# Dividing attention's sums by features: transfers and wide reciprocals in place of TensorE transposes, in a fused block of one core

## The reference

```python
x = x + 0.5 * ffn(layernorm(x))
x = x + attention(layernorm(x))
x = x + 0.5 * ffn(layernorm(x))

def attention(x):                      # 16 heads of 16 features
    q, k, v = split(lora_linear(x, Wq, ...)), split(...), split(...)
    scores = einsum('bhqd,bhkd->bhqk', q, k) * 16 ** -0.5
    attn = softmax(scores, axis=-1)
    out = einsum('bhqk,bhkd->bhqd', attn, v)
    out = merge_heads(out)             # B x 1024 x 256
    return lora_linear(out, Wo, bo, Bo, Ao)
```

## Time and profile before

| | |
|---|---|
| median of three runs | 830.17 us (829.87 to 831.24) |
| the profiled execution | 832.18 us, of which its span is 830.4 us |
| PE busy in the span | 806.1 us, 97% |
| DVE busy | 681.9 us, 82% |
| ACT busy | 474.0 us, 57% |
| POOL busy | 194.2 us, 23% |
| chain that ended last | PE 85%, DVE 8%, ACT 4%, issue 3%, DMA 1% |

### The profile page before, as it was taken

One profiled execution on the slowest core, in us unless ns is written; L12 is line 12 of the kernel. 1 busy time (PEld: TensorE's weight loads), 2 busy tenths in 40 slices (PEclk: granted clock), 3 DMA queues, 4 the chain that ended last, 5 costly groups with the idle time before them and its releaser, 6 DMA issues.

```text
span 830.4 us, 14316 instructions
## 1 busy us (share of the span) xinstructions
PE 806.1 (97%) x5424; PEld 516.8 (62%) x5424; DVE 681.9 (82%) x1127; ACT 474.0 (57%) x900; POOL 194.2 (23%) x206
## 2 busy tenths in 40 slices
PE   5989999999999999999999999999999999999997
PEld 4868788888876433333333434443358888888886
DVE  4997888787599999999999888889846977876865
ACT  4543433432432788888888888888863333333322
POOL 1450112410011033333332322143430201120100
PEclk9999999999999999999999999999999999999999
DMA  8110000000050242223333222210000000000000
GB/s 278 39 39 1 0 1 1 2 1 0 1 90 1 40 79 54 40 39 65 65 65 64 41 40 40 59 33 27 16 12 1 1 2 26 0 26 1 1 25 26
DMA packets 19333, 27.87 MB, mean 34 GB/s; under 512 B 4608, under 2 KB 13632, under 8 KB 19264
## 3 DMA queue, kind: packets, MB, share of 16 engines
q1 hardware_dynamic: 18592, 26.30, 14.5%
q10 hardware_dynamic: 672, 0.66, 0.3%
HBM read 12.09 MB, written 2.10 MB: 17 GB/s over the span
## 4 chain that ended last, share of the span: by engine, by line
PE 85%; DVE 8%; ACT 4%; issue 3%; DMA 1%; DVEq 0%; ACTq 0%; POOL 0%
PE front_ps L1668 17%; PE front_ps L1649 14%; PE max_ps L1609 6%; PE ffn_gate_ps L49 5%; PE ffn_gate_ps L51 5%; PE ffn_gate_ps L50 5%; PE ffn_out_ps L756 5%; PE ffn_out_ps L757 5%; PE ffn_out_ps L760 5%; PE ffn_up_ps L49 3%; PE ffn_up_ps L51 3%; PE ffn_up_ps L50 3%; ACT probs L1799 2%; PE ffn_mix_ps L735 2%; DVE ffn_hidden_lo L1119 1%
## 5 line engine op out<-in xcount | busy, mean ns | idle before, releaser
L1879 DVE TENSOR_REDUCE maxima<-max_ps 128x2 f32<-128x1024 f32 x256 | 311.1, 1223 | 29.3 <-PE max_ps L1609 26.8
L1799 ACT ACTIVATE probs<-front_ps 128x512 f32<-128x512 f32 x512 | 277.5, 597 | 38.9 <-PE front_ps L1649 29.1
L882 ACT ACTIVATE ffn_tanh<-ffn_gate_ps 128x512 f32<-128x512 f32 x96 | 57.4, 598 | 219.0 <-PE ffn_gate_ps L51 219.0
L1668 PE MATMUL front_ps<-probs,values 128*32 128x256 f32 x2048 | 163.4, 391 | 4.4 <-ACT mixed_t L1804 4.0
L1128 DVE SCALAR_TENSOR_TENSOR ffn_gated<-ffn_tanh,ffn_gate_ps 128x512 f32<-128x512 f32 x96 | 65.8, 685 | 61.2 <-ACT ffn_tanh L882 60.8
L1668 PEld LDWEIGHTS front_ps<-probs,values 128*32 128x32 f32 x2048 | 40.8, 108 | 95.5 <-issue 55.7
L1649 PE MATMUL front_ps<-q_stack,k_stack 49*128 49x512 f32 x256 | 94.6, 446 | 0.0
L1609 PE MATMUL max_ps<-ffn_xlo,ffn_xhi 48*128 48x512 f32 x256 | 93.9, 447 | 0.0
L1549 POOL TENSOR_TENSOR inverse_sum<-turned,minus_one 128x16 f32<-128x16 f32 x15 | 43.7, 2916 | 207.4 <-ACT turned L1811 207.4
L1649 PE MATMUL front_ps<-ffn_xhi,ffn_xlo 49*128 49x512 f32 x256 | 91.4, 455 | 0.0
L1609 PE MATMUL max_ps<-k_stack,q_stack 48*128 48x512 f32 x256 | 88.2, 455 | 0.6 <-DVE maxima L1879 0.4
(11 more groups left out here) (209 smaller groups left out, 1296.2 us busy)
## 6 DMA issues: line engine op xcount, KB each, us to landing
q_stack<-block SPq DMA_DIRECT2D x48, 64.0 KB, 2.3
ffn_xhi<-block SPq DMA_DIRECT2D x48, 64.0 KB, 2.3
ffn_xlo<-block SPq DMA_DIRECT2D x48, 64.0 KB, 2.3
k_stack<-block SPq DMA_DIRECT2D x42, 64.0 KB, 2.3
x_sb<-in_x SPq DMA_DIRECT2D x3, 512.0 KB, 9.3
out<-x_sb SPq DMA_DIRECT2D x3, 512.0 KB, 2.9
ffn_out_rows<-in_down SPq DMA_DIRECT2D x4, 256.0 KB, 5.9
weights_again<-in_gate SPq DMA_DIRECT2D x2, 512.0 KB, 3.6
```

Source lines behind the costliest of these rows:

```text
L1668: mm = pe.matmul(mixed_ps[strip:strip + STRIP, at:at + HALF // 2], values[g % SLOTS][:, kt, j, :], probs[:, (g * KEY_TILES + kt) % PROBS, ...
L1799: act.activation(probs[:, tile % PROBS, j, half * HALF:(half + 1) * HALF], score_ps[:, n % RING, :], ACT.Exp, scale=SCORE_SCALE).then_inc( ...
L1879: v.reduce_max(maxima[:, g % 2, m // 2, m % 2, :], max_ps[:, m % 2, :, :], axis=AXIS_X).then_inc(pair_max, 1)
```

## The change

The mix is no longer turned. `values` now has 16 columns of v and 16 columns of ones, so that each strip of the mix has 16 rows of features and the same sum in 16 further rows. Once the mix is copied out, SyncE issues eight transfers per group (`move_on_sync`): four bring the features' rows into `attn_out`, which now has features in its rows, and four the sums' rows to the same rows of a buffer `sums` of 128 x 1024. When four groups are there, VectorE takes the reciprocal of all the sums in one instruction, before the maxima of groups 6, 10 and 14 (`invert_on_vector`), and GpSimd multiplies (`normalize_on_gpsimd`). The last four groups are divided by VectorE in two halves of 512 columns, behind units 0 and 2 of the second FFN (`divide_last_on_vector`). The output product reads `attn_out` as it is. `turn_out`, `copy_turned`, `write_out`, `turn_on_tensor`, `columns_of` and `LastMix` go.

```diff
+    MOVES = 4
-            self.columns = sb("o_columns", [P, 2, KT, PAIR_TILES, P])
+            self.sums = sb("o_sums", [P, SEQ])
...
+    def move_on_sync(self, sp, g, mixed):
+        sp.wait_ge(self.mixed_out, g + 1)
+        for half in range(2):
+            at = slice(half * HALF, (half + 1) * HALF)
+            for j in range(2):
+                strip, to = (j * 2 + half) * 2 * HD, (g % SLOTS * 2 + j) * HD
+                sp.dma_start(self.rows_of(g)[to:to + HD, at], mixed[strip:strip + HD, :]
+                             ).then_inc(self.moved[half], 16)
+                sp.dma_start(self.sums[to:to + HD, at], mixed[strip + HD:strip + 2 * HD, :]
+                             ).then_inc(self.moved[half], 16)
+    def invert_on_vector(self, v, s):
+        for half in range(2):
+            self.wait_moved(v, half, (s + 1) * SLOTS)
+        v.reciprocal(self.sums[:, :], self.sums[:, :]).then_inc(self.inverted, 1)
+    def normalize_on_gpsimd(self, pool, s):
+        rows = self.rows_of(s * SLOTS)
+        pool.wait_ge(self.inverted, s + 1)
+        pool.tensor_tensor(rows, rows, self.sums[:, :], ALU.mult).then_inc(self.normalized, 1)
+    def divide_last_on_vector(self, v, half):
+        at, before = slice(half * HALF, (half + 1) * HALF), GROUPS // SLOTS - 1
+        rows = self.rows_of(GROUPS - 1)[:, at]
+        self.wait_moved(v, half, GROUPS)
+        v.reciprocal(self.sums[:, at], self.sums[:, at]).then_inc(self.inverted, 1)
+        v.wait_ge(self.inverted, before + half + 1)
+        v.tensor_tensor(rows, rows, self.sums[:, at], ALU.mult).then_inc(self.normalized, 1)
...
# second FFN: TensorE, ScalarE, VectorE
         def output_product(p):
-            pe.wait_ge(project.columns_done, p + 1)
+            pe.wait_ge(project.normalized, GROUPS // SLOTS + p // 2)
...
-            if u == 0 and not first:
-                pe.wait_ge(rows_out, JT // 2 - 1)
-                last.turn_on_tensor(pe, out_ps[:, 0, :], ident[:, :])
-            if pair_beside(u, 0) in (0, 1):
-                turn_attention(pair_beside(u, 0))
...
-            last.write_on_vector(v)
             v.wait_ge(keep["x_biased"], CHUNKS)
         for u in range(UNITS_ALL):
             unit(u)
             if u:
                 low_part(u - 1)
+            if not first and u in (0, 2):
+                project.divide_last_on_vector(v, u // 2)
...
# attention: SyncE
+            def move_out(g):
+                if g % SLOTS == 0:
+                    sp.wait_ge(values_in, g + SLOTS)
+                    if g:
+                        sp.wait_ge(project.normalized, g // SLOTS)
+                project.move_on_sync(sp, g, mixed[:, :])
             for g in range(GROUPS - 1):
+                if g:
+                    move_out(g - 1)
...
+            for g in (GROUPS - 2, GROUPS - 1):
+                move_out(g)
# attention: TensorE and ScalarE
-                    if kt == OUT_TURN_AT and g:
-                        turn_out(g - 1)
...
-                    if kt == TURN_ROWS_AT and 0 <= g - FIRST_PAIR_AT < NORM_PAIRS:
-                        attention_rows(g - FIRST_PAIR_AT)
...
             def copy_mixed(g):
                 act.wait_ge(probs_used, (g + 1) * KEY_TILES)
+                if g:
+                    for half in range(2):
+                        project.wait_moved(act, half, g)
# attention: VectorE and GpSimd
             for g in range(GROUPS):
+                if g % SLOTS == 2 and g > SLOTS:
+                    project.invert_on_vector(v, g // SLOTS - 1)
...
+                if g % SLOTS == SLOTS - 1:
+                    project.normalize_on_gpsimd(pool, g // SLOTS)
```

More of the change, by code:

```diff
@@ L750, in down @@
                     pe.wait_ge(rows_out, JT // 2)
-                    pe.wait_ge(last.copied, 1)
             x_hi, x_lo = hidden_hi[:, u % SPLIT_RING, :], hidden_lo[:, u % SPLIT_RING, :]
@@ L924, in _ @@
                 raw.copy_update_on_scalar(act, 2, update_banks[2])
-            if u == 0 and not first:
-                last.copy_on_scalar(act, out_ps[:, 0, :])
             for c, i in routing_beside(u - 1):
```

147 lines of the change are left out of this document (26 added, 121 removed).

## The result

| | kernel before | changed kernel |
|---|---|---|
| median of the runs, us | 830.02 (829.77 to 831.24, 4 runs) | 880.99 (869.87 to 891.32, 4 runs) |
| ratio, undisturbed runs | | 1.0492, 95% interval 1.0472 to 1.0513 |
| profiled execution, us | 832.18 | 869.87 |
| its span, mean granted clock of TensorE | 830.4, 0.996 | 868.0, 0.954 |

The change costs 40 us or more, where 21.3 were forecast and the range ended at 864. The direction was right, the size was not. The four executions of the changed kernel took 869.87, 873.13, 888.85 and 891.32 us at a mean granted clock of 0.954, 0.953, 0.930 and 0.928.

What follows compares the result with a forecast made beforehand. TensorE was taken to set the pace in attention and the second FFN. Terms -11.4 + 17.5 + 7.5 + 5.2 + 2.5 = +21.3 us gave a median of 851.5 us, likeliest case 846 to 857, 8 in 10 839 to 864.

Steps and rivals of the forecast that it cites:

- point 3: Attention: after each of the three long pauses TensorE's clock halves, costing 2.5 us each, 7.5 us lost; bounds 0 and twice that.
- point 4: Second FFN: waits for the half reciprocals lose 5.2 us net of turns gone; one clock drop adds 2.5 us.
- the clock stays up: Rival: no clock loss in attention or the second FFN, so +11.3 us, 841.5 us; chance 0.17.
- Point 1: Attention: the transposes go, 0.60 us each time on TensorE, 19 times, 11.4 us gained.
- SyncE itself is not late: Attention: SyncE's eight issues end some 13 us after the group's start, the maxima's rows are issued 17.9 us after it.
- Point 2: Attention, groups 4, 8 and 12: VectorE's reciprocals of 1024 columns take 6.6 us each; 6.5, 6.2 and 4.8, together 17.5 us lost.
- The half microsecond per group: Opening, attention: VectorE, busy 19.64 of 21 us, was said to have about half a microsecond per group to spare.
- the plain rate: Rival: a reciprocal of 1024 columns runs at the plain rate, 1.2 us, giving -9.7 us, 820.5 us; chance 0.08.
- eight slots to a column: Rival: at 8.3 ns per column a reciprocal of 1024 columns takes 8.6 us, giving 859 us; chance 0.10.
- The transfers that land late: Rival: transfers land after 4.6 us instead of 2.3, three waits in attention and one in the FFN grow, 860 us; chance 0.10.

Runs made afterwards that it cites:

- e7: e6 with the last four groups divided in quarters of 256 columns, behind units 0, 3, 11 and 20 of the second FFN: 823.34 us, ratio 0.9919.
- e3: Kernel before, with two idle reciprocals of 512 columns of ones on VectorE before the maxima of groups 6, 10 and 14: 873.58 us median.
- e6: Changed kernel, sums of groups 0 to 11 moved once, inverted by one reciprocal of 64 columns per four groups, repeated through DRAM: 828.62 us, ratio 0.9983.
- e2: Changed kernel with each of attention's three reciprocals cut into eight pieces of 128 columns, one behind every second reduction: 877.91 us median, ratio 1.0548.
- e12: Changed kernel with 24 products of the 128x128 identity on TensorE ahead of one score in groups 4, 8 and 12: 845.84 us median, ratio 1.0189.
- e11: Changed kernel with the first score of key tile 6 done twenty-five times on TensorE in groups 4, 8 and 12: 874.62 us median, ratio 1.0484.

## Why the forecast was right in sign and wrong in size

**The step that failed is point 3, the clock**, and with it the clock's part of point 4. The mechanism was right, and the size of this term was not. It said "I count 2.5 after each: 7.5 us", from one pause in the first FFN, with 0 and 15 us as its ends. In the profiled execution of the changed kernel the clock was low for 61 us in attention (24, 17 and 20, summed over windows of 2 us). Some 10 of these lay in the stops themselves, where TensorE had nothing to lose; 19, 15 and 17 us came after it had its work back. A step then took 2.16 us instead of 1.24, so a share of 0.43 is lost, which gives 22 us.

The same can be measured directly, by the maxima's rows, which SyncE issues once per group. The changed kernel's, around groups 4, 8 and 12:

```profile
370.51 1.38 SPq L1444 DMA_DIRECT2D q_stack<-max_rows  x2
405.14 1.37 SPq L1444 DMA_DIRECT2D ffn_xhi<-max_rows  x2
...
467.29 1.37 SPq L1444 DMA_DIRECT2D q_stack<-max_rows  x2
501.72 1.38 SPq L1444 DMA_DIRECT2D ffn_xhi<-max_rows  x2
...
568.55 1.38 SPq L1444 DMA_DIRECT2D q_stack<-max_rows  x2
600.80 1.37 SPq L1444 DMA_DIRECT2D ffn_xhi<-max_rows  x2
```

They are 34.63, 34.43 and 32.25 us apart. In e7, with no long wait there and the clock at 1.00, the same three distances are 20.37, 22.29 and 20.38. Less TensorE's waits of 5.86, 5.62 and 4.34, that leaves 8.4, 6.5 and 7.5 us for the clock: 22.4 where 7.5 were counted, and 7 above the upper end of 15. In the second FFN some 11 us of work ran at half the clock, which an estimate at a share of a half prices at 5 to 6 us, where 2.5 were counted. In all the clock took 28 us, not 10.

The whole account of the two profiled executions, span against span and rounded; attention is taken from the first to the last issue of maxima's rows:

| part | forecast, us | measured, us |
|---|---|---|
| turns gone up to group 14, with the stop by the late rows of group 2 | -10.8 | -9.0 |
| TensorE's three stops in attention | 17.5 | 15.8 |
| the clock in attention | 7.5 | 22.4 |
| behind that: the last group's turn and the second FFN, with its clock | 7.1 | 9.9 |
| up to attention | 0 | -1.6 |
| together | 21.3 | 37.6 |

The -1.6 is no effect of the change: the first FFN was at half the clock for 3.4 us in this execution and for 6.8 in the profiled one of before. Without the 28 us the profiled execution would have taken about 842 us, where the forecast's other terms give 843.5. The rival "the clock stays up" stood at 841.5 for the median. So all the other terms together were right to about 2 us, with small errors that cancel.

A second way to see the clock's part: over the four executions of the changed kernel the time rises by 7.6 us for each 0.01 that the mean clock is lower, and over e3's four by 7.4. Carried to 0.996, the clock of the kernel before, the changed kernel would take 839 us. That is well outside the clocks seen, and it also takes off the low clock inside the stops, where nothing was lost, so it comes out a few us too low.

**Point 1, the turns.** The rows of the maxima are issued at 350.14 and 370.51 in the changed kernel, 20.37 us apart, and at 351.89 and 372.85 in the one before, 20.96: 0.59 us less in such a group, with 0.60 forecast:

```profile
350.14 1.38 SPq L1444 DMA_DIRECT2D q_stack<-max_rows  x2
370.51 1.38 SPq L1444 DMA_DIRECT2D q_stack<-max_rows  x2
```

```profile
351.89 1.38 SPq L1482 DMA_DIRECT2D q_stack<-max_rows  x2
372.85 1.38 SPq L1482 DMA_DIRECT2D q_stack<-max_rows  x2
```

The first pair is SyncE's of the changed kernel, the second that of the kernel before. Of the other distances between these issues, those with one turn less are shorter by 0.57 to 0.59, and the three from group 9 to group 12, with two turns less, by 1.15 to 1.21. The two from group 0 to group 2 gained nothing together (42.28 us for 41.91): there the stop of 1.47 us stands. "SyncE itself is not late" was worked out from group 8 and does not hold in group 1.

**Point 2, the reciprocals.** 6.553 us for 6.6, and 5.86, 5.62 and 4.34 us of TensorE's waiting in groups 4, 8 and 12, for 6.5, 6.2 and 4.8 of loss. The half microsecond per group that the opening gives VectorE to spare in attention is misread: 21 less 19.64 is 1.36. No term of the sum uses it. The line through the two narrow rows, 166 ns for 2 columns and 0.25 us for 16, held to 1024 columns. With it fall two rivals: the plain rate (1.2 us), and eight slots to a column. The latter was a reading of the Trainium skill's "VectorE: DVE Perf Modes" (section on the fixed hardware budget); this trace has 6.4 ns per column in all, not 8.3. The transfers that land late, the third rival, did not happen either: 2.3 us of waiting in all three places together.

**Point 4, the second FFN.** The output product started after 2.96 us of waiting, and the turn behind unit 2 after 3.36; a pause of 3.7 and a loss of 3.9 were forecast. But half the clock began in both pauses, and not in one.

**What in the working led to it.** One stretch of another stage stood for a quantity, how long the clock stays down, that had no row in attention at all; the range around it was drawn from that one number. The first FFN's pauses are followed by 128x512 work. Attention's scores behind its pauses are 48 and 49 rows deep, and the clock rose after 8 to 50 us there. That the shape of the work is what delays the rise is argued from this difference alone, and as the same work of attention took 8 us in one place and 50 in another, it cannot be all of it. The cause of the long stay stays open.

## What to carry to other kernels

A long instruction on an engine that TensorE waits for costs its own length only if TensorE's clock survives the stop; price the clock by a pause in the same kind of work, and where there is none, give it a range of several times the one that you have. When a stretch gets slower though every engine is "busy", look at the granted clock and the number of matmuls in a window before looking for a new wait. And where repeated data is to be inverted or looked up, do it on one copy, spread over the partitions, and repeat it afterwards by a transfer: 0.55 us of VectorE in the place of 6.55 was the difference between losing 40 us and losing nothing (e6), and with the quarters of e7 7 us were gained.

## What the runs showed of the hardware that was not expected

- Half the clock lasted 8 to 19 us after TensorE's work came back in attention of the changed kernel and e3, but 50 us in e2 (402 to 454) and about 48 in e12 (314 to 362), against 5 to 6 us in the first FFN of the kernel before and the second of the changed one. Why one stretch ends after 8 us and a like one after 50 stays open; no run here separates it.
- A busy TensorE can lose its clock: in e11 it fell at 384.6 us, 5.5 us after a row of 49x512 products with nothing beside them began, though TensorE did not pause. The same stop with 128x128 products kept it. The Trainium skill's "TensorE: Matmul & The Clock Gate" (Part 1, on the clock gate) says that the throttled state is the default and that activity releases it. The trace agrees in so far as the clock falls where TensorE stands (at 371.8 us in group 4 of the changed kernel, 1.2 us into the stop); these two runs add that being busy in time did not keep it.
- The reciprocal costs about 0.15 us and 6.25 ns per column at every width seen: 166 ns for 2 columns, 554 for 64, 944 for 128, 1748 for 256, 3350 for 512, 6553 for 1024; a copy of 1024 columns takes 694 ns.
